# Graph-attention layer on one core: sixteen idle products at the start, two sets of bias columns moved

## The reference, cut to what matters

```python
nx = _ln(x, ln1_g, ln1_b)
q = (nx @ wq + bq).reshape(b, s, H, HD).transpose(0, 2, 1, 3)
k = (nx @ wk + bk).reshape(b, s, H, HD).transpose(0, 2, 1, 3)
v = (nx @ wv + bv).reshape(b, s, H, HD).transpose(0, 2, 1, 3)
bias = jnp.where(adj_matrix > 0, 0.1 * edge_attr_matrix * adjf, -jnp.inf)[:, None]
scores = jnp.einsum('bhqd,bhkd->bhqk', q, k) / np.sqrt(HD) + bias
attn = jax.nn.softmax(scores, axis=-1)
out = jnp.einsum('bhqk,bhkd->bhqd', attn, v)
x1 = residual + (out @ wo + bo)
n2 = _ln(x1, ln2_g, ln2_b)
mlp = jax.nn.gelu(n2 @ w1 + b1, approximate=False) @ w2 + b2
return x1 + mlp
```

## Time and profile before

| | |
|---|---|
| median of 3 runs | 1409.81 us (1408.53 to 1409.89) |
| the profiled execution | 1407.88 us |
| its span in the trace | 1406.1 us |
| granted TensorE clock, mean over the span | 0.988 |
| TensorE busy | 1354.4 us (96%) |
| VectorE busy | 1190.3 us (85%) |
| ScalarE busy | 1135.5 us (81%) |
| GpSimd busy | 559.5 us (40%) |

### The profile page before, as it was taken

One profiled execution on the slowest core, in us unless ns is written; L12 is line 12 of the kernel. 1 busy time (PEld: TensorE's weight loads), 2 busy tenths in 40 slices (PEclk: granted clock), 3 DMA queues, 4 the chain that ended last, 5 costly groups with the idle time before them and its releaser, 6 DMA issues.

```text
span 1406.1 us, 34020 instructions
## 1 busy us (share of the span) xinstructions
PE 1354.4 (96%) x11580; PEld 1165.4 (83%) x11580; DVE 1190.3 (85%) x2002; ACT 1135.5 (81%) x3336; POOL 559.5 (40%) x553
## 2 busy tenths in 40 slices
PE   7579999999999999999999999999999999999998
PEld 6468888888888888888888888888888888888876
DVE  3888988888898888898888899888889888889862
ACT  3678888888889888888888888988888988888753
POOL 3343334443334443333444333444333444433321
PEclk9889999999999999999999999999999999999999
DMA  4343334443333434333444333443433344433330
GB/s 150 113 142 122 126 123 138 145 137 131 126 121 125 153 127 146 130 112 126 143 142 142 119 128 123 134 152 127 140 130 115 119 153 141 142 120 121 101 118 23
DMA packets 147256, 180.15 MB, mean 128 GB/s; under 512 B 13584, under 2 KB 130576, under 8 KB 147216
## 3 DMA queue, kind: packets, MB, share of 16 engines
q1 hardware_dynamic: 147216, 179.63, 39.3%
HBM read 95.69 MB, written 83.89 MB: 128 GB/s over the span
## 4 chain that ended last, share of the span: by engine, by line
PE 91%; ACT 5%; DVE 2%; DMA 1%; issue 1%; POOL 0%; SPq 0%; ACTq 0%; DVEq 0%; POOLq 0%
PE work L376 27%; PE work L378 25%; PE work L377 25%; PE area L432 6%; PE work L478 4%; PE work L452 4%; ACT qk_all L653 2%; ACT soft L610 1%; PE work L383 1%; ACT late_memory L677 0%; DVE soft L839 0%; DVE wa_raw L851 0%; ACT late_memory L688 0%; DMA wa_raw<-in_L_gnn_wq 0%; DVE soft L815 0%
## 5 line engine op out<-in xcount | busy, mean ns | idle before, releaser
L610 ACT ACTIVATE soft<-soft,nmax 128x128 f32<-128x128 f32 x1024 | 396.8, 394 | 5.1 <-DVE nmax L823 4.7
L1015 POOL TENSOR_TENSOR ve<-mv,eps 128x4 f32<-128x4 f32 x64 | 13.0, 203 | 771.0 <-DVE mv L888 664.7
L376 PE MATMUL work<-w_hi,hid_parts 128*128 128x256 f32 x1024 | 295.4, 288 | 1.4 <-ACT late_memory L688 1.1
L378 PE MATMUL work<-w_hi,hid_parts 128*128 128x256 f32 x1024 | 286.1, 279 | 0.0
L377 PE MATMUL work<-w_lo,hid_parts 128*128 128x256 f32 x1024 | 285.9, 279 | 0.0
L924 DVE TENSOR_TENSOR hid_parts<-late_memory,hid_parts 128x512 fp32r<-128x512 f32 x256 | 224.9, 880 | 21.8 <-ACT hid_parts L698 21.6
L688 ACT ACTIVATE late_memory<-work,b_col 128x512 f32<-128x512 f32 x256 | 171.9, 684 | 69.9 <-PE work L378 53.8
L376 PE MATMUL work<-nt_hi,w_hi 128*128 128x512 f32 x512 | 211.7, 414 | 3.9 <-DVE nt_lo L914 3.8
L376 PEld LDWEIGHTS work<-w_hi,hid_parts 128*128 128x128 f32 x1024 | 191.9, 187 | 12.0 <-DVE xt_lo L914 5.8
L377 PE MATMUL work<-nt_lo,w_hi 128*128 128x512 f32 x512 | 201.3, 393 | 0.0
L378 PE MATMUL work<-nt_hi,w_lo 128*128 128x512 f32 x512 | 200.5, 392 | 0.0
(11 more groups left out here) (93 smaller groups left out, 3074.2 us busy)
## 6 DMA issues: line engine op xcount, KB each, us to landing
moved_blocks<-wa_raw SPq DMA_DIRECT2D x128, 512.0 KB, 2.7
probt<-moved_blocks SPq DMA_DIRECT2D x512, 128.0 KB, 2.9
xin<-in_x SPq DMA_DIRECT2D x32, 512.0 KB, 3.9
out<-res SPq DMA_DIRECT2D x128, 128.0 KB, 2.1
adj_in<-in_adj SPq DMA_DIRECT2D x32, 256.0 KB, 2.9
res<-in_L_gnn_w SPq DMA_DIRECT2D x1, 1024.0 KB, 9.6
late_memory<-in_L_gnn_w SPq DMA_DIRECT2D x1, 1024.0 KB, 12.1
wa_raw<-in_L_gnn_wq SPq DMA_DIRECT2D x1, 256.0 KB, 3.9
```

Of the source, the lines that this page charges most:

```text
L376: pe.matmul(o, lhs_hi, rhs_hi, start=first, stop=False)
L378: return pe.matmul(o, lhs_lo, rhs_hi, start=False, stop=last)
L610: a = act.activation(soft[:, b % 2, h, :], soft[:, b % 2, h, :], ACT.Exp, bias=nmax[:, b % 2, h:h + 1], accum_out=rsum[:, b % 2, h:h + 1])
```

## The change

There are three parts. Sixteen float32 products of the identity with itself go to a part of PSUM that nothing reads (`spare`, the unused columns of the first scores bank), as soon as the identity is there. `early_columns` is called right behind them, ahead of the first turning. The sixteen products for b1 leave `late_columns` and stand in `late_rows`, behind the two products for `wout`; VectorE adds b1 there, behind `bo_rows`, and the waits on `b1_ready` move accordingly.

```diff
+AWAKE = 16
...
+        spare = area[:, 0, DC * P:(DC + 1) * P]
...
                 for m in range(DC):
-                    offset_column(mixed[:, m:m + 1], wa_raw[:, 2, :, m * P:(m + 1) * P], ln_cols[:, 1, :])
+                    mm = offset_column(mixed[:, m:m + 1], wa_raw[:, 2, :, m * P:(m + 1) * P], ln_cols[:, 1, :])
+                mm.then_inc(v_cols_ready, 1)
+
+            def late_rows():
+
+
+                pe.wait_ge(wa_loaded[3], 16)
+                pe.wait_ge(bv_spread, 1)
+                for c in range(DC):
+                    pe.matmul(wout, bv_wide[:, c, :], wa_raw[:, 3, c, :],
+                                   start=(c == 0), stop=(c == DC - 1))
                 pe.wait_ge(w1_loaded, 16)
                 for m in range(FC):
                     mm = offset_column(mixed[:, DC + m:DC + m + 1], w1_raw[:, :, m * P:(m + 1) * P],
                                        ln_cols[:, 3, :])
-                mm.then_inc(vb_cols_ready, 1)
-
-            def late_rows():
-
-
-                pe.wait_ge(wa_loaded[3], 16)
-                pe.wait_ge(b1_ready, 1)
-                pe.wait_ge(bv_spread, 1)
-                for c in range(DC):
-                    mm = pe.matmul(wout, bv_wide[:, c, :], wa_raw[:, 3, c, :],
-                                   start=(c == 0), stop=(c == DC - 1))
                 mm.then_inc(bo_ready, 1)
 
             pe.wait_ge(ident_ready, 1)
+            for _ in range(AWAKE):
+                pe.matmul(spare, ident[:, :], ident[:, :], start=True, stop=True)
+            early_columns()
...
                 if step.at_first(off) and b == 0:
                     pe.wait_ge(bo_added, 1)
+                    pe.wait_ge(b1_ready, 1)
...
-                if kind == "xt" and c == DC - 1 and step.at_first(off):
-                    early_columns()
...
-                dve.wait_ge(vb_cols_ready, 1)
+                dve.wait_ge(v_cols_ready, 1)
                 dve.tensor_tensor(bv_col[:, :], mixed[:, 0:DC], bias_in[:, 2, :], ALU.add)\
                    .then_inc(bv_ready, 1)
-                dve.tensor_tensor(b1_col[:, :], mixed[:, DC:DC + FC], b1_in, ALU.add)\
-                   .then_inc(b1_ready, 1)
...
                 dve.tensor_tensor(bo_rows[:, :], wout, bo_rows[:, :], ALU.add).then_inc(bo_added, 1)
+                dve.tensor_tensor(b1_col[:, :], mixed[:, DC:DC + FC], b1_in, ALU.add)\
+                   .then_inc(b1_ready, 1)
```

More of the change, by code:

```diff
@@ L221, in gnn_block @@
         bqk_ready = sem("bqk_ready")
-        vb_cols_ready = sem("vb_cols_ready")
+        v_cols_ready = sem("v_cols_ready")
         bv_ready = sem("bv_ready")
```

## The result

The changed kernel takes 1405.89 us (median of 9 runs, 1403.34 to 1408.07), the kernel before, run beside it, 1409.81 us (9 runs, 1407.91 to 1412.75). The ratio is 0.9973, with a 95% interval of 0.9962 to 0.9984. By the medians that is 3.9 us, 0.28% faster; by the ratio 2.3 to 5.4 us. The prediction was 1406.0.

The account below looks back on a forecast made before the run. TensorE was taken as the bound (busy 96% of the span), so gains before 89 us carry through. Terms -1.66 - 0.4 - 1.8 = -3.86, taken as -3.8, gave 1404.1 us profiled, median 1406.0; range 1403.8 to 1409.2 us.

Parts of the forecast that it names:

- That the early steps carry through to the end: First 89 us: a microsecond gained there is one at the end, if nothing between eats it.
- The idle products and moved columns cost nothing: Kernel start: both end at 8.3 to 9.1 us, covered by the wait for `xhat` until 10.03 us.
- The third rival: Kernel start: idle products slow at 0.43 us a record, kernel 4.9 us slower, 1414.7 us; chance 0.04.
- First gain: Before the query/key stage: bq/bk columns leave the path, first product at 14.15 for 15.81 us, -1.66 us.
- Second gain: Query/key stage: clock falls beforehand but rises 4.1 us behind the stage's start in place of 4.9, -0.4 us.
- Third gain: Query/key stage to first scores: b1's columns leave, `values` half 1 and scores run at upper clock, -6.9 us.
- Price: Behind `wout`: b1's columns take 4.6 us, transposes at lower clock +0.45; together +5.05, net of third gain -1.8 us.
- the clock term: Query/key stage: the rise comes 4.1 us behind its start in place of 4.9, -0.4 us.
- The first: From the idle products on: the clock holds, 1.9 us more gain, 1404.1 us; chance 0.12.
- The second: Between 40 and 89 us: lower-clock stretches eat the gain, 1 to 3 us more there, 1408.2 us; chance 0.26.
- The fourth: Kernel start: not on the path at all, the long part starts no earlier, 1409.8 us; chance 0.06.

Follow-up runs that it names:

- the fill: Changed kernel plus idle products behind the bq/bk columns and behind the first transposes, up to the query/key stage: 1403.00 us, ratio 0.9949.
- b1's columns moved out: Changed kernel with b1's columns moved behind the first step's last query/key product, into spare columns of the first scores bank: 1402.12 us, ratio 0.9947.
- both: Changed kernel with idle products through all gaps up to the query/key stage and b1's columns behind its last product: 1398.81 us, ratio 0.9927.

## Why the prediction was right, point by point

**That the early steps carry through to the end** held best. The gain stands at 4.11 us at `xt_hi` of group 1, at 4.44 at the start of the full stage and at 4.5 at the end. The 0.33 us between the first two came from VectorE's first scaling of probabilities, which took 1.24 us on the chain in place of 1.57. It goes with the place of b1's columns: in the five profiles that have them between `wout` and the transposes the scaling took 1.22 to 1.23 us, with GpSimd's `ebias<-adj_in` beside it, and in the other five 1.55 to 1.56, with `tenth<-adj_in` beside it. Why the one slows it and the other does not was not tested.

**The idle products and moved columns cost nothing:** they end at 9.2 us, the sum said 8.3 to 9.1. (In two other profiles with the same start they end at 9.6 and 9.8, still ahead of `xhat`.) The pitch of float32 products was rightly read from the columns and not from the 0.43 us: 32 records in 5.8 us. The third rival is out.

**First gain, -1.66 us:** 15.81 to 13.90 us is 1.91. The transposes of half 1 no longer bind at the upper clock, which the term left out; VectorE takes both halves of `xt_lo` back to back, from 12.47 us. In three other profiles with these columns moved, in which most or all of the transposes ran at the lower clock, the product came at 14.40 to 14.47 us, a gain of 1.3 to 1.4.

**Second gain, -0.4 us: this term failed, and had the wrong sign.** The fall ahead of the query/key stage was foreseen; but the rise, taken 4.1 us behind its start from rows with 3.3 and 4.9, came 5.8 us behind it (13.90 to 19.71), and the stage took 9.63 us in place of 9.23: 0.4 us lost. Two rises were too few to bound a third. In two kernels with the same work ahead of the stage the rise came 3.2 and 6.1 us behind its start (14.40 to 17.64, and 14.47 to 20.60) and the stage took 8.48 and 9.82 us: over these three the mean is 9.3, no gain at all, and one execution can fall on either side. Leaving the idle products out, or using them alone, showed that they bring nothing that was measured.

**Third gain, -6.9 us:** it was right to 0.35 us; from bv's columns to VectorE's first addition of edges were 9.91 us (25.04 to 34.95) and are 3.36 (23.53 to 26.89): -6.55.

**Price, +5.05 us:** the columns took 3.49 us (29.80 to 33.29), the lower bound, not the 4.6 taken. The clock fell at 33.36, behind them and not in their midst. Four other profiles have the same order: without the idle products the columns took 3.49 us too (30.30 to 33.79), and in the three others 4.57, 4.43 and 4.68 (30.53 to 35.10, 27.04 to 31.47 and 29.39 to 34.07). The 4.6 was thus a fair size, and missed in this execution. The +0.45 for the transposes at the lower clock held, at 0.93 us for 0.45.

The profile's own sum is -1.91 + 0.40 - 6.55 + 3.97 = -4.1 us, the gain at `xt_hi`. It paid 1.1 us less than the price said, lost 0.8 at the clock term, and was 0.1 off in the other two together. The mechanism was right; that -3.8 met a median of -3.9 so closely is in part luck, since errors cancelled, and since the prediction carried a forecast for one execution over to the median by an offset of 1.9 us. The range is not the sum of its bounds either: -1.66, -2.3 and -3.4 together would reach to 1402.4 us, and the range stops at 1403.8.

The Trainium skill's advice (TensorE: Matmul & The Clock Gate, "Why this matters for your kernels") to warm up, and to leave no long idle gaps between bursts, fits in its direction: the warm-up by itself measured 1.0002, and with all gaps filled the stage ran 2.6 us shorter. The gaps that the Trainium skill warns of there are longer than the 2.26 us behind which the clock fell in the kernel with the idle products alone; here the measurement decides.

**The rivals.** The first did not happen here, and happens when the gaps are filled. The second did not happen in the profile after, where the late stretches at the lower clock moved along with their work. It did in four of the eight other kernels: from the `values` products (91.71 us before) to the first product of the MLP (97.92) it took 9.8 us with b1's columns moved alone, 7.9 with the fill, 8.5 with b1's columns moved out and 8.4 with both, for 6.2 before and after. So 1.7 to 3.6 us of what the start had won were lost there, up to 0.8 of them in a longer wait for ScalarE and the rest at the lower clock. Its chance of 0.26 was no exaggeration, and the profiled execution of the change was a lucky one in this. The fourth is refuted: the interval of the change excludes 1, and the gain made by 34 us is there at the end.

## What to carry to other kernels

Work that nobody needs yet should leave the path before one tries to speed up its clock: of the change, the two moves carry what was measured (0.20% without the idle products, 0.27% with them, the same within the error), each of them a part, and the idle products nothing that was measured. (The bq/bk columns moved with nothing else were not run.) Idle products paid here only where they kept TensorE nearly busy up to the work that they were for and started nothing later: sixteen that ended 2.3 us before the next transposes bought nothing, fourteen more in the gaps bought 2.6 us of TensorE time, and sixteen more in one block ahead held the clock too but gave back what they won. And a moved piece has still a price at its new place: ask once more who waits behind it there, since the same columns, moved a second time into real slack, were worth 2.4 to 3.8 us more, nearly the whole change again.

## What the runs showed of the hardware

In all ten profiles the clock fell in the midst of b1's 32 records, whose moving operand has a single column, or at most 0.5 us behind them. They took from 3.63 to 5.63 us for the same work, by where among them the fall came. That their single column is the reason was not tested. The same dense row of idle products, begun at 1.52 us each time, was followed by the rise at 4.69 us in one execution and at 7.69 in another. ScalarE began `xhat`, which releases everything after it, between 9.16 and 10.15 us in the ten profiles, though no experiment edits its work ahead of that. And in four of the ten the clock fell once more at about 1340 us, far from anything that the kernels do differently, for 3.4 us in three and 6.8 in one; these four ended 0.9 to 2.0 us less far ahead of the kernel before than they were at the first product of the MLP, or further behind it. One kernel's executions scatter by 4.7 us (the changed one's), as much as this change is worth; how much of that is due to each of these was not separated. A single profile therefore shows which waits have gone, and only the medians and ratios of many runs show what that is worth.
